# Normalising both token tiles of an image on ScalarE in the first router of a two-layer MetaFormer kernel

## The reference

```
t = t + _L0_ffn_ref(_ln_t(t), router_w, gate_w, up_w, down_w)

def _ln_t(v, eps=1e-05):
    m = mean(v, -1); s = var(v, -1)
    return (v - m) / sqrt(s + eps)

# in _L0_ffn_ref:
logits = flat @ router_w.T                      # 8 experts
topk_prob, topk_idx = top_k(softmax(logits), 2)
...
y = (silu(flat @ gate_w[e].T) * (flat @ up_w[e].T)) @ down_w[e].T
```

## Time and profile before

| what | value |
|---|---|
| runs | 1091.94, 1095.45 (median), 1097.87 us |
| profiled execution: its own time | 1092.11 us |
| profiled execution: span from the first to the last instruction | 1090.3 us |
| mean granted TensorE clock | 0.887 of full speed |
| busy: PE, DVE, ACT, POOL | 938.1, 615.7, 546.7, 269.6 us |
| the block of the first router | 66.6 to 119.4 us of the span |

### The profile page before, as it was taken

One profiled execution on the slowest core, in us unless ns is written; L12 is line 12 of the kernel. 1 busy time (PEld: TensorE's weight loads), 2 busy tenths in 40 slices (PEclk: granted clock), 3 DMA queues, 4 the chain that ended last, 5 costly groups with the idle time before them and its releaser, 6 DMA issues. The chain is left out here.

```text
span 1090.3 us, 19992 instructions
## 1 busy us (share of the span) xinstructions
PE 938.1 (86%) x5742; PEld 797.4 (73%) x5742; DVE 615.7 (56%) x1722; ACT 546.7 (50%) x1360; POOL 269.6 (25%) x274
## 2 busy tenths in 40 slices
PE   6866469999999999997288998998746899998998
PEld 2753368888888888886266766776525899997898
DVE  6888743232323232322676778667887455555776
ACT  5526444343444444433356555554225566667774
POOL 0000022121212121210763220000000444443776
PEclk9656659999999999999589999998655799999999
DMA  9644411111111111111843121102330444444654
GB/s 385 261 140 170 155 30 54 54 53 55 51 57 49 59 49 59 49 47 42 274 138 102 59 77 60 40 20 78 119 114 18 133 140 138 137 131 134 181 156 145
DMA packets 63236, 114.74 MB, mean 105 GB/s; under 512 B 9698, under 2 KB 43124, under 8 KB 62132
## 3 DMA queue, kind: packets, MB, share of 16 engines
q1 hardware_dynamic: 49908, 77.77, 20.3%
q0 software_dynamic: 12960, 35.41, 11.4%
q10 hardware_dynamic: 288, 0.47, 0.1%
HBM read 74.01 MB, written 39.59 MB: 104 GB/s over the span
## 5 line engine op out<-in xcount | busy, mean ns | idle before, releaser
L600 POOL DMA_INDIRECT experts_rows_sb<-h_rows,choices x142 | 134.0, 944 | 667.4 <-POOLq L428 338.6
L795 DVE TENSOR_TENSOR experts_a_sb<-experts_a_sb,experts_bankU 128x512 f32<-128x512 f32 x71 | 48.9, 689 | 224.1 <-PE experts_bankU L184 224.1
L746 ACT ACTIVATE experts_a_sb<-experts_bankG 128x512 f32<-128x512 f32 (+1 forms) x142 | 69.7, 491 | 92.7 <-PE experts_bankG L184 92.5
L737 ACT ACTIVATE experts_hT<-experts_bankH 128x256 fp32r<-128x256 f32 x142 | 54.2, 382 | 90.0 <-PE experts_bankH L663 89.8
L759 ACT ACTIVATE experts_y_sb<-experts_bankY 128x256 f32<-128x256 f32 x142 | 54.7, 385 | 86.4 <-PE experts_bankY L181 66.6
L1186 POOL DMA_INDIRECT attn_y<-y_rows,choices x64 | 65.8, 1028 | 109.0 <-DVE x_res L1626 56.9
L916 POOL DMA_INDIRECT shared_y<-y_rows,choices x64 | 69.6, 1087 | 37.8 <-POOLq L555 18.6
L181 PE MATMUL experts_bankY<-down_plain,experts_aT_plain 128*128 x284 | 72.9, 379 | 0.0
L187 DVE TENSOR_TENSOR experts_aT<-experts_bankA,experts_aT 128x256 fp32r<-128x256 f32 x142 | 59.6, 419 | 23.0 <-ACT experts_aT L754 23.0
L670 PE MATMUL experts_bankA<-konst_sb,experts_a_sb 128*128 128x128 f32 x426 | 70.0, 273 | 1.7 <-DVE experts_aT L187 1.7
L187 DVE TENSOR_TENSOR experts_hT<-experts_bankH,experts_hT 128x256 fp32r<-128x256 f32 x142 | 59.7, 421 | 18.6 <-ACT experts_hT L737 18.6
(11 more groups left out here) (376 smaller groups left out, 2761.2 us busy)
## 6 DMA issues: line engine op xcount, KB each, us to landing
y_rows<-experts_y_sb SPq DMA_DIRECT2D x142, 128.0 KB, 1.7
h_rows<-xn SPq DMA_DIRECT2D x32, 256.0 KB, 2.3
mix_xT<-in_xt SPq DMA_DIRECT2D x4, 1024.0 KB, 12.0
x_res<-in_x SPq DMA_DIRECT2D x4, 1024.0 KB, 13.8
gate_raw<-in_L_ffn_gate_w SPq DMA_DIRECT2D x2, 2048.0 KB, 13.1
up_raw<-in_L_ffn_up_w SPq DMA_DIRECT2D x1, 4096.0 KB, 25.0
x_rows<-x_res SPq DMA_DIRECT2D x16, 256.0 KB, 2.5
x_res<-x_rows SPq DMA_DIRECT2D x8, 512.0 KB, 4.6
```

The lines of the kernel that those rows point to most:

```text
L600: nc.gpsimd.indirect_dma_start(rows[t % DEPTH][:, :], None, h_dram, bass.IndirectOffsetOnAxis(ap=ids_i[:, t:t + 1], axis=0)).then_inc(s_ro ...
L746: nc.scalar.activation(a_sb[i % RING][:, :], bankG[i % RING][:, 0:hidden], ACT.Silu if gate is not None else ACT.Relu).then_inc(s["act"], 1)
L795: nc.vector.tensor_tensor(a_sb[i % RING][:, :], a_sb[i % RING][:, :], bankU[i % RING][:, 0:hidden], ALU.mult).then_inc(s["a"], 1)
```

## The change

The first tile's normalisation is taken off DVE. ACT's `normalise(n)` has a loop over both tiles, and only the second of the two instructions signals, on one semaphore `xn` that takes the place of `xn_dve` and `xn_act`. PE's `transpose(n)` and SP's store wait for that one semaphore. DVE's waits of the removed function (for `rstd`, for the transposition and for the store of image n-2) go with it; ACT has had the same waits.

```diff
-                        sp.wait_ge(s["xn_dve"], n + 1)
-                        sp.wait_ge(s["xn_act"], n + 1)
+                        sp.wait_ge(s["xn"], n + 1)
...
-                        t = n * HALVES + 1
-                        nc.scalar.activation(xn[n % RING][:, C:2 * C], x_tile(t), ACT.Identity, bias=shift[:, t:t + 1],
-                                             scale=rstds[:, t:t + 1]).then_inc(s["xn_act"], 1)
+                        for h in range(HALVES):
+                            t = n * HALVES + h
+                            last = nc.scalar.activation(xn[n % RING][:, h * C:(h + 1) * C], x_tile(t), ACT.Identity, bias=shift[:, t:t + 1],
+                                                        scale=rstds[:, t:t + 1])
+                        last.then_inc(s["xn"], 1)
...
-                        pe.wait_ge(s["xn_dve"], n + 1)
-                        pe.wait_ge(s["xn_act"], n + 1)
+                        pe.wait_ge(s["xn"], n + 1)
...
-                    def normalise(n):
-                        dve.wait_ge(s["rstd"], n * HALVES // CHUNK_T + 1)
-                        if n >= RING:
-                            dve.wait_ge(s["transposed"], n - RING + 1)
-                            dve.wait_ge(s_stored[n % RING], n // RING * 16)
-                        t = n * HALVES
-                        nc.vector.tensor_scalar(xn[n % RING][:, 0:C], x_tile(t), rstds[:, t:t + 1], shift[:, t:t + 1],
-                                                ALU.mult, ALU.add).then_inc(s["xn_dve"], 1)
...
-                    normalise(0)
                     for n in range(IMAGES):
-                        if n + 1 < IMAGES:
-                            normalise(n + 1)
                         for piece in halves.share(n):
                             halves.low(dve, piece)
```

More of the change, by code:

```diff
@@ L264, in router_front @@
             with ExitStack() as on:
-                s = {n: sem(f"{tag}_{n}") for n in ("var", "sqrt", "rstd", "xn_dve", "xn_act", "transposed", "copied", "routed", "logits_sb", "logits", "chain", "spilled")}
+                s = {n: sem(f"{tag}_{n}") for n in ("var", "sqrt", "rstd", "xn", "transposed", "copied", "routed", "logits_sb", "logits", "chain", "spilled")}
                 s_stored = [sem(f"{tag}_stored{b}") for b in range(RING)]
```

## The result

The change makes the kernel slower by a little: 1095.12 us against 1091.91, each the median of 19 runs; the ratio is 1.0033, with a 95% interval from 1.0019 to 1.0046, that is +3.6 us (2.1 to 5.0) on 1091.91. The forecast was +3.1 us, 0.28%.

What follows compares the result with a forecast made beforehand. The prediction took a loop over DVE and ACT (normalisations, weight copies, statistics, root) to pace the first router's block. Terms of 1.25 + 0.96 + 0.91 = 3.1 us on 1095.45 gave 1098.6 us, range 1094.0 to 1102.0.

Steps and rivals of the forecast that it cites:

- The second tile: On ACT, each added normalisation behind a first one takes 0.49 us from start to start.
- A steady round: Two rounds, each 0.48 us longer: later ACT copies delay DVE, freed DVE normalisations give part back; 0.96 us together.
- the slack at the root: ACT's idle time ahead of the square root: 1.78 us before, 0.80 left after four added tiles.
- The first round: Up to the block's first steady round: end moves by 0.98 to 1.47 us, taken as 1.25.
- The tail: After the last deviations: image 15's pair and the last store come later, adding 0.91 us.
- the sum's lower bound: Whole block: 1.75 us, if the last store lands sooner and DVE's selection decides the end.
- Merged waits: SP and PE wait for one semaphore instead of two; gain taken as nothing.
- DVE's work is the bound: Rival, chance 0.08: in the rounds, waits for ACT vanish and DVE's freed time gives 3.9 us; 1091.6 us.
- nothing reaches the end: Rival, chance 0.10: loss in the rounds is absorbed by the block's end, 0 to 1 us; 1095.5 to 1096.5.
- A late store: Rival, chance 0.16: a slow store landing holds back image 15 by 2.2 us, 5.3 us in all; 1100.8 us.
- The rule: Skill page giving additions and multiplications to VectorE; by it alone, all sixteen tiles on the path, 2.9 us slower.
- The sum: Whole block: 1.25 + 0.96 + 0.91 = 3.1 us slower, 0.28%.

Runs made afterwards that it cites:

- late_images: Kernel before, with both tiles on ACT only for images 2 and 3 of each group of four; 1.0014 of the time before.
- early_images: Kernel before, with both tiles on ACT only for images 0 and 1 of each group of four; 1.0007 of the time before.
- two_sems: Changed kernel with two semaphores for the pair again, both set by ACT, PE and SP waiting for both; 1.0028 of the time before.
- before_ahead: Kernel before, with ACT's rounded copy of the next weight piece ahead of its next normalisation; 0.9985 of the time before.
- mix_ahead: Kernel before, with copies ahead of normalisations and both tiles on ACT only for images 2 and 3 of each group except the last; 0.9947 of the time before.
- early_again: The kernel of early_images run once more with more rounds, beside the changed kernel; 1.0025 of the time before.
- tail_only: Kernel before, with both tiles on ACT only for the last four images (12 to 15); 1.0024 of the time before.

## Why the prediction was right, point by point

*The second tile.* Taken at 0.49 us; four in a row last 2.08 us, so (2.08 - 0.60) / 3 = 0.49.

*A steady round.* Forecast 12.85 us, measured 12.84 and 12.86. Each step of it can be read: the copy of piece 8 started 0.98 us later, DVE's wait for it grew to 1.19 us (forecast 1.3), the slack at the root is 0.80 us as worked out, and DVE's two last pieces (2.53 us for the two, one behind the other) give back part of the freed normalisations. late_images and early_images show the two signs of that sum apart, -0.51 and +0.98 us of a round; they add up to 0.47, the change's 0.48. (ACT's list printed under the change begins with image 9, not 8: its first row waits for `moe0_stored1`, the buffer of the odd images. Image 8's tiles and piece 7 stand ahead of it, and so two added tiles stand ahead of piece 8.)

*The first round.* Forecast 0.98 to 1.47 us, taken as 1.25; measured 12.40 - 11.29 = 1.11. The middle was too much: image 0's store, issued 0.49 us later, landed only 0.12 us later behind the first `deviations` (77.62 - 72.16 = 5.46 us, and 77.09 - 71.75 = 5.34 before). The two added tiles behind it make the other 0.98, and so the copy of piece 2 starts 1.11 us later, at 81.13 - 72.16 = 8.97 us and not at 79.61 - 71.75 = 7.86; before and with the change:

```profile
79.61 1.04 ACT L218 ACTIVATE up_high<-up_raw 128x1024 fp32r<-128x1024 f32 x1
```
```profile
81.13 1.04 ACT L218 ACTIVATE up_high<-up_raw 128x1024 fp32r<-128x1024 f32 x1
```

The four normalisations ahead of the first piece, which the forecast named first, don't end this round: late_images has two there, as before, and its first round grows by the same 1.11 us.

*The tail.* Forecast +0.91 us, measured +0.58, and +0.30 in the second execution: this is the term of the sum that was mis-sized. Image 15's pair and its store came as worked out:

```profile
117.22 0.37 SPq L280 DMA_DIRECT2D h_rows<-xn  x1
```

That is 6.96 us after the last `deviations`, against 6.13 before; forecast 7.03. What the forecast made too long is the way from this issue to the next block, which it kept at the 5.48 us of before. In the second execution the stores end the block as they did before (SP, which waits for them, then waits 0.2 us for the other engines in both, and 0.5 in the first execution of the change), and it is 121.02 - 116.05 = 4.97 us, in two_sems 5.04. Why these stores land sooner was not tried; the two ahead of the last are issued 1.63 us apart (113.82 and 115.45), before 0.98 (110.97 and 111.95).

In the first profile this way took 5.23 us (to 122.45), and there DVE's selection set the end: done at 121.55 + 0.36 = 121.91, it was only 0.54 us ahead of the next block, not 1.47, the case that the sum's lower bound had allowed for. The selection itself began 7.38 us after `deviations`, 5.87 before, because it waited 4.05 us for PE's logits. PE's product for image 11 (L354) and the logits that the selection waits for (L361), before and with the change:

```profile
109.90 0.63 PE L354 MATMUL moe_bankL<-moe_xT,router_sb 128*32 128x128 f32 x8 [0.68 <-ACT moe_xT L309]
...
113.30 0.33 PE L361 MATMUL moe_logits<-konst_sb,choices 128*128 128x128 f32 x1
```
```profile
112.86 1.07 PE L354 MATMUL moe_bankL<-moe_xT,router_sb 128*32 128x128 f32 x8 [0.31 <-ACT moe_xT L310]
...
117.28 0.33 PE L361 MATMUL moe_logits<-konst_sb,choices 128*128 128x128 f32 x1
```

The product starts 2.60 us after `deviations`, not 2.11: that is the second tile of image 12, ahead of it on ACT. From there to the logits the same instructions take PE 4.42 us, not 3.40. So of the selection's 1.51 us 0.49 is the change's tile, and 1.02 came with PE, which ran at the lower clock level in most of that stretch, as the last section shows; the forecast had no term for it.

*Merged waits.* Taken as nothing; two_sems shows nothing.

*The rivals.* That DVE's work is the bound fell: its sign was rounds under 12.37 us, and they are 12.85. DVE's work comes near to pacing a round only where the copies were moved ahead: it is busy for 10.43 of 10.93 us in before_ahead and for 9.75 of 10.26 in mix_ahead. That nothing reaches the end fell with the block's 2.65 us and an interval that excludes 1. A late store fell too: image 15 waited 0.20 us for it and started 116.10 - 113.82 = 2.28 us behind its issue, and the sign was 2.5.

*The rule.* The page "ScalarE: Activation LUTs" of the Trainium skill, section "Rules for kernel authors", gives multiplications and additions to VectorE; here the sign agrees for all sixteen tiles, but the trace decides by place: with the eight tiles of late_images the steady rounds got 0.51 us shorter.

*The sum.* 3.1 us forecast; 2.65 in the block of the first profile, 2.37 in the second, and +3.6 (2.1 to 5.0) in the time of the runs, which holds both. The rest of the first profile's 6.5 us belongs to that execution: behind the block it took 1096.8 - 122.45 = 974.35 us, in the second execution of the same kernel 1090.2 - 121.02 = 969.2, and before 970.9. The interval is too wide to rule out a us or two behind the block.

*The time.* The difference was right, the time less so: 1098.6 us was forecast and 1095.12 measured, 3.5 less. The forecast counted from 1095.45, the median of the three runs shown; the median of 19 runs of the kernel before is 1091.91. That 1095.12 still lies in the stated range, 1.1 us above its lower end of 1094.0, is owed to the width of the range. And runs of this kernel tell less than 0.5% from no change: with 19 of each, 0.33% is clear of it.

## What to carry to other kernels

Before moving an instruction to a less busy engine, look what stands behind it in that engine's list and who waits for that: here the same tile cost 0.49 us in front of a copy that another engine awaited, and nothing in front of an idle stretch. The longest wait on the list (PE's for `xn`) isn't the one that paces; the one to follow is the loop in which two engines wait for each other in turn. And where such a loop is found, try the order of the list before the split of the work: putting work that is ready ahead of work that waits gave 2.1 us a round, four times what the change cost.

## What the runs showed of the hardware

The tail of one and the same kernel took 13.10 us in one execution of early_images and 11.68 in the other, with the rounds before it equal. Busy times in the 7.38 us behind the last `deviations`, with the granted clock in third place from the end, in the kernel before, the change, early_images and early_again, in this order:

```profile
107.79:115.17 7.38, 6.11 (x58) 3.70 (x54) 4.15 (x9) 6.09 (x12) 0.00 (x0) 0.94 0.67 235
```
```profile
110.26:117.64 7.38, 5.89 (x40) 3.90 (x41) 1.23 (x1) 7.15 (x15) 0.00 (x0) 0.60 0.58 205
```
```profile
110.04:117.42 7.38, 6.58 (x43) 4.12 (x41) 2.05 (x3) 6.21 (x12) 0.00 (x0) 0.50 0.62 217
```
```profile
109.66:117.04 7.38, 6.57 (x54) 4.26 (x52) 2.52 (x5) 6.55 (x14) 0.00 (x0) 0.68 0.62 217
```

TensorE was granted 0.94 of its clock before, 0.60 with the change, 0.50 throughout (the level of 1.2 GHz) in the slow tail of early_images and 0.68 in the other. At the lower level four transpositions of an image take 1.06 us, at the higher 0.67, as these two rows of the changed kernel show:

```profile
114.13 1.06 PE L342 MATMUL moe_bankT<-konst_sb,xn 128*128 128x128 f32 x4
...
116.12 0.67 PE L342 MATMUL moe_bankT<-konst_sb,xn 128*128 128x128 f32 x4
```

In this tail the last images go through PE one after the other to the selection. From the product for image 11 to the selection's logits PE took 117.94 - 112.64 = 5.30 us in the slow tail and 116.17 - 112.27 = 3.90 in the other, with no wait in between: that is 1.40 of the 1.42 us. No run set the clock by itself, so that the clock alone does it is read from these rows and not tried. In the rounds it doesn't show: the changed kernel's two steady rounds were granted 0.50 and 0.63, in the second execution 0.63 and 0.50, and all four took 12.84 to 12.87 us; there PE waits for `xn`.

The other surprise is how much code that no kernel here changed varies from one execution to the next: behind the block it took between 968.4 us (1087.4 - 118.98, tail_only) and 976.6 (1099.7 - 123.14, early_images), three times what the change is worth. That is why the block was read and not the span, and of the block the steady rounds above all.
